# Four transformer layers on one core: the common order of 536 steps laid out anew, and buffer waits named by their own readers

## The reference

```python
x = x + tanh(gx[0]) * L0_xattn(ln(x), ctx)      # 16 heads, two softmaxes each, their difference
x = x + tanh(gf[0]) * L0_ffn(ln(x))             # three cycles of a small network that turns x
x = x + tanh(gx[1]) * L1_xattn(ctx, ln(x), mask) # 8 heads, keys from context and x
x = x + tanh(gf[1]) * L1_ffn(ln(x))             # 2 shared and 8 routed experts, best two
x = x + tanh(gx[2]) * L2_xattn(ln(x), ctx, ctx) # 16 heads
x = x + tanh(gf[2]) * L2_ffn(ln(x))             # attention, then 8 experts, best two
x = x + tanh(gx[3]) * L3_xattn(ln(x), ctx, ctx) # one head of 256
x = x + tanh(gf[3]) * L3_ffn(ln(x))             # two products with values rounded to 8 bits
```

## Time and profile before

| | |
|---|---|
| time of the runs | 5605.34, 5625.49, 5621.25 us; median 5621.25 |
| the profiled execution: its own time, its span | 5613.03 us, 5611.2 us |
| mean granted TensorE clock | 0.901 of full speed |
| busy: PE, DVE, ACT, POOL | 4673.8, 2894.8, 1919.8, 95.3 us |
| weight loads on PE | 3499.8 us, beside the matmuls |
| chain that ended last | PE 59%, DVE 27%, ACT 6%, issue 4%, DMA 3%, POOL 1% |

### The profile page before, as it was taken

How to read it: one execution, slowest core, us unless ns; L and a number is a source line. 1 busy time by engine, 2 the same in 40 slices (tenths; PEclk the granted TensorE clock), 3 DMA queues, 4 the chain that set the end, 5 groups by cost and what they waited for, 6 DMA issues and landing times.

```text
span 5611.2 us, 74711 instructions
## 1 busy us (share of the span) xinstructions
PE 4673.8 (83%) x29184; PEld 3499.8 (62%) x29184; DVE 2894.8 (52%) x7495; ACT 1919.8 (34%) x3132; POOL 95.3 (2%) x180
## 2 busy tenths in 40 slices
PE   2888878989789897898878988789887898878988
PEld 1566755667557585575855758557585575845757
DVE  4555455554555545555455454454544555455554
ACT  2433324333243333424234242342423424243242
POOL 0000000000000000000000000000000000000000
PEclk9899988989889898898978989789897998989989
DMA  6000210003000030000200002001020010200002
GB/s 254 1 15 22 105 43 1 15 22 119 29 1 23 14 121 27 1 29 23 106 27 1 29 28 101 27 1 36 23 98 27 3 34 23 98 28 12 25 23 102
DMA packets 49467, 241.04 MB, mean 43 GB/s; under 512 B 4800, under 2 KB 17088, under 8 KB 27328
## 3 DMA queue, kind: packets, MB, share of 16 engines
q1 hardware_dynamic: 49088, 235.92, 11.4%
HBM read 214.93 MB, written 20.97 MB: 42 GB/s over the span
## 4 chain that ended last, share of the span: by engine, by line
PE 59%; DVE 27%; ACT 6%; issue 4%; DMA 3%; POOL 1%; SPq 0%; DVEq 0%; ACTq 0%; another core or an unknown queue 0%
PE w L434 14%; PE w L444 9%; DVE mx L1049 7%; PE o L577 6%; PE w L693 6%; PE w L424 4%; PE w L685 4%; PE w L500 2%; PE o L570 2%; PE w L534 2%; ACT oth L805 2%; DVE stats L982 1%; PE w L549 1%; PE w L589 1%; DVE rs L995 1%
## 5 line engine op out<-in xcount | busy, mean ns | idle before, releaser
L843 ACT ACTIVATE pt<-w 128x1024 f32<-128x1024 f32 x640 | 653.3, 1023 | 560.1 <-PE w L500 316.7
L1049 DVE TENSOR_REDUCE mx<-w 128x4 f32<-128x1024 f32 x512 | 593.6, 1218 | 169.0 <-PE w L483 153.8
L577 PE MATMUL o<-pt,va 128*32 128x256 f32 x4096 | 556.0, 408 | 18.7 <-ACT pt L843 18.7
L805 ACT ACTIVATE oth<-w,res 128x256 f32<-128x256 f32 x656 | 263.5, 474 | 718.6 <-PE w L685 603.8
L434 PE MATMUL w<-xnT,stream 128*128 128x256 f32 x1792 | 426.2, 388 | 6.2 <-ACT xnT L797 6.2
L434 PEld LDWEIGHTS w<-xnT,stream 128*128 128x128 f32 x1792 | 348.0, 195 | 57.1 <-issue 7.9
L685 PE MATMUL w<-qsp,ksp 128*128 128x256 f32 x2048 | 350.9, 289 | 0.0
L577 PEld LDWEIGHTS o<-pt,va 128*32 128x32 f32 x4096 | 206.9, 113 | 191.6 <-issue 64.2
L483 PE MATMUL w<-ksp,qsp 32*128 32x256 f32 (+1 forms) x2048 | 257.9, 395 | 76.1 <-DVE mx L1049 43.8
L1019 DVE SCALAR_TENSOR_TENSOR x<-w,gate,x 128x256 f32<-128x256 f32 x512 | 224.1, 479 | 170.1 <-PE w L693 147.8
L434 PE MATMUL w<-xnT,res 128*128 128x256 f32 x896 | 280.5, 464 | 36.5 <-ACT xnT L797 27.6
(11 more groups left out here) (258 smaller groups left out, 8372.0 us busy)
## 6 DMA issues: line engine op xcount, KB each, us to landing
stream_lo<-split SPq DMA_DIRECT2D x64, 1024.0 KB, 4.8
ksp<-split SPq DMA_DIRECT2D x64, 1024.0 KB, 6.9
stream<-in_moe_dram SPq DMA_DIRECT2D x80, 384.0 KB, 3.1
stream<-in_resident_dram SPq DMA_DIRECT2D x8, 2048.0 KB, 9.0
va<-in_moe_dram SPq DMA_DIRECT2D x8, 1024.0 KB, 9.9
split<-ksp SPq DMA_DIRECT2D x8, 1024.0 KB, 5.6
split<-qsp SPq DMA_DIRECT2D x8, 1024.0 KB, 8.0
stream<-in_resident_dram SPq DMA_DIRECT2D x8, 1024.0 KB, 4.6
```

The lines of the kernel that those rows point to most:

```text
L577: mm = pe.matmul(o[g:g + 32, 0:T], by_heads(plan, s)[:, kt, plan.v_of(h), :], pt[:, n % EXPS, a * 512 + kt * T:a * 512 + (kt + 1) * T], st ...
L805: h = act.activation(dst[:, c, :], w[:, c * T:(c + 1) * T], func, bias=bias[:, c:c + 1], **more)
L843: act.activation(pt[:, n % EXPS, :], w[:, :], ACT.Exp, scale=scale).then_inc(S["s_P"], 1)
L1049: dve.tensor_reduce(mx[s][:, :, 2 * u:2 * u + 2].rearrange("p t a -> p a t"), w[:, :].rearrange("p (a t k) -> p a t k", a=2, t=TT), AX_X, ...
```

## The change

The string `ORDER` is replaced. It has the same digits, each as often as before, so every step is still done once and in the order of its own list; only the interleaving of the ten lists differs. No operation, shape or transfer is added or taken away. Three waits change: PE's wait before an `obank` is written again names the `pv` step that wrote it two items before and waits for that item's own signal; ACT's wait before a `pt` place is written again names the `exp` step that wrote it two before and waits for the `pv` that reads it; and `l3.k` waits on ACT until the last `f2.exp` of its slot is filled. `keep_item` takes the number of the buffer from the count of started items in place of that of ended ones.

```diff
 ORDER = (
-    "1016110156106000006006000005000600050550550005000500050500000550050550500500505050005000500555055055"
...
+    "6661111011605060000000000050006000050055055505000550050550000050555000000005505000005500050205550555"
+    "5055555555055055555505555550575005500050005500550702050050555505055000505050770525005050005200505005"
+    "0500050055005055050050050550555050500550050055550555555555550053505580500505080550550055005500505055"
+    "5085550530508530350000505005050050500055055000055005000500050500500505005550550555550505505050050500"
+    "0505005505005555050550500550050050000500050555055555055505505500504555555090505505509505050050550500"
+    "505050550550405550505005500550050050"
 )
...
+EXP_STEPS = steps_named(*SIGNALS["s_P"])
+ITEM_STEPS = list(ITEM)
...
                 if plan.item_starts(u) and i >= 2:
-                    pe.wait_ge(S["s_oT"], i - 1)
+                    last, ls, lu = ITEM_STEPS[i - 2]
+                    pe.wait_ge(*after("s_oT", last, ls, lu + PLANS[last[:2]].units_per_item - 1))
...
                 if n >= EXPS:
-                    act.wait_ge(S["s_pv"], n - EXPS + 1)
+                    last, ls, lu = EXP_STEPS[n - EXPS]
+                    act.wait_ge(*after("s_pv", last[:2] + ".pv", ls, lu))
...
-                bank = obank[(COUNT["s_oT"][plan.name + ".pv", s, u] - 1) % 2]
+                bank = obank[(ITEM[plan.name + ".pv", s, i * plan.units_per_item] - 1) % 2]
...
                         o = 0 if what == "q" else 2
+                        if what == "k":
+                            full(act, "f2.exp", s, F2.units - 1)
                         biased(qz[s][:, o:o + 2, :], full(act, step, s), W_["l3_b" + what], FC).then_inc(S["s_qk3"], 1)
```

More of the change, by code:

```diff
@@ L195 @@
 ORDER = (
-    "1016110156106000006006000005000600050550550005000500050500000550050550500500505050005000500555055055"
[L197 to L201, removed]
+    "6661111011605060000000000050006000050055055505000550050550000050555000000005505000005500050205550555"
+    "5055555555055055555505555550575005500050005500550702050050555505055000505050770525005050005200505005"
+    "0500050055005055050050050550555050500550550055555555555550053505580500505080550550055005500505055005"
+    "5085550530508530350000505005050050500055055000055005000500050500505005550550555550505505050505050500"
+    "0505005505005555050550500550050050000500050555055555055505550500504555555090505505509505050050550500"
+    "505050550550405550505005500550050050"
 )
```

## The result

Four runs of the changed kernel took 5525.89, 5526.36, 5531.95 and 5526.96 us, median 5526.66, beside 5616.51 for the kernel before on the same chip. The ratio is 0.9843, 95% interval 0.9822 to 0.9863: the change is faster by 1.6%, 90 us. The forecast was 5552 us; direction and range hold, the size was 61 us forecast and 90 measured.

A forecast was written before the change was run, and what follows sets the result against it. No engine is full; the order bounds the stages with waits. Terms 3.5 + 2.7 + 0 + 1.4 + 0 - 0.5 + 0.5 = 7.6 us a pass, 61 in eight, from 5613.0 to 5552 us; range 5460 to 5630.

The forecast's parts named there:

- Waits at nothing: The three changed buffer waits: same counts as the old ones or fills already done, so no time won or lost.
- Start of the pass, 3.5: Pass start to the first exp: 3.5 us a pass won, 1.9 of it from the clock; bounds 0 and 5.5.
- Signs: Profile after: `0.l0.xT` wait near 1 us, `0.l0.max:0` some 23 us after the first transpose, `shift` waits below 1 us.
- Layer 0, 2.7: Layer 0 to `f0`: a `pt` wait (1.2 us) and the `0.l0.oT` wait (1.5) go, 2.7 won.
- `f0` and the head of `l1`: 0: `0.f0.xT` to `0.l1.max:0`: two waits of 9.4 us go, new ones of 9.2 come, so 0; ends +9.4 and -14.6.
- first rival: `f0` chains overlap, no new wait shows: 9.4 us more a pass, 17.0 in all, 5477 us; chance 0.22.
- `l1`, 1.4: In `l1`, `1.l1.xT` and `1.l1.max:0` get more cover, 0.7 us each: 1.4 won a pass; bounds 0 and 1.4.
- `f1`, layer 2, `f2`: 0 in sum: `f1` begins 0, layer 2 loses 0.5 us, layer 2 to `f2` wins 0.5 a pass.
- third rival: Interleaved `f0` chains block each other: stretch of 89.0 us or more, say 96; 5669 us, slower; chance 0.14.
- second rival: Where DVE sets the pace, gains return as idle PE: start 0, layer 2 -2.5, `f2` 0; 5600 us; chance 0.18.

The follow-up runs named there:

- turn_late: Changed kernel with `1.f0.turn:0`, `1.f0.cT:1` and `1.f0.h1:1` moved behind slot 0's `f0.add` and `l1.ln`: 5630.91 us, ratio 1.0031 to the kernel before.
- old_waits: Kernel before, its three buffer waits kept, with the new `ORDER` alone: 5526.07 us, ratio 0.984 to the kernel before.
- start_only: Splice: new order for the first 89 steps (to `0.l0.exp:15`), the old order from there: 5594.82 us, ratio 0.996 to the kernel before.
- cln_moved: Changed kernel with `1.l1.cln` moved from ahead of `1.l0.norm` to behind `1.f0.ln`, and `1.l1.cT` behind `0.f0.t:1`: 5526.68 us, ratio 0.9843 to the kernel before.
- max_later: Changed kernel with the 19 steps behind `0.f2.shift:0` put back in their old sequence: 5568.2 us, ratio 0.9897 to the kernel before.
- l2_old: Changed kernel with the old order for steps 251 to 337 (`f1` and head of layer 2): 5493.17 us, ratio 0.9782 to the kernel before.
- front_only: Splice: new order for steps 0 to 250, the old order from there: 5475.18 us, ratio 0.9758 to the kernel before.

## Why the prediction was right, and where it failed

**The direction** was right, and its reason too: the order, and not an engine's work, bounds the stages with waits, and most of the waits named as dear went or shrank. `turn_late` shows that the place of the turn in the order makes its wait: 13.3 us there, 6.0 before the change, none after it.

**The total** came within the range in part by luck, since errors of opposite sign meet in it: `f0` won 8.4 us more than was said, while `f1`, layer 2 and `f2` lost 4.5 and the second context 1.3. A pass takes 679.3 us in the mean (682 was said).

**Waits at nothing:** right, as far as `old_waits` can tell.

**Start of the pass, 3.5:** 3.9 by the table, but its row ends at `1.l0.pv:0` and so holds the 1.2 us wait on `pt` that the prediction had counted under layer 0. Up to the first exponential, as the prediction had it, the start won 3.4: 1.3 idle and 2.1 busy time, near the 1.6 and 1.9 that the prediction gave without the clock and to the clock alone. With the second context's wait, which the prediction had not looked at, 2.1 to 2.2 are left: it gave the transfers no price, but the new order asks first for the context that is loaded second. Signs: `0.l0.xT` waits 1.27 (about 1 was said); the first maximum at 24.05 us in the third pass, 23.5 in the mean (23 was said). Not right: shift waits below 1 us; they are 2.30 in layers 0 and 2. And the clock did not rise through both stretches: 0.79 in the first, 0.50 in the second, where it cost little.

**Layer 0, 2.7:** the two waits went as said, on `pt` (1.2) and at `0.l0.oT` (1.5), 2.7 together. Another 2.1 us up to `1.l0.pv:12` were won in faster matmuls, which the prediction had not counted, and 0.7 were lost between the first exponential and `1.l0.exp:1`.

**"`f0` and the head of `l1`: 0"** is the step that failed. Its mechanism was right, its terms were mis-sized. The two long waits went (9.4). The new ones were given 9.2 and measure 5.9: `1.l0.oT` 3.06 in place of 4, `0.f0.cT:1` nothing in place of 1.6, `1.f0.h2:1` 0.86 in place of 2.1, `0.l1.xT` and `0.l1.vl` 0 and 1.96 in place of 1.5 together. And waits whose end I had not listed went as well: before `0.f0.h1:1` 2.41 to 0.14 us, `0.l1.xT` 1.28 to 0, `0.l1.q` 1.11 to 0, 4.7 in all. 9.4 + 4.7 - 5.9 = 8.2. The list leaves smaller waits out; all idle time together fell by 7.7 and busy time by 0.7, the 8.4 of the ledger. The stretch from `0.f0.xT` to `0.l1.max:0` alone is 75.66 us where the prediction counted 81.4, so 5.8 are won inside it and the rest beside it. The slow matmuls mostly changed places: `1.l1.vc` fell from 5.76 to 3.60 us, `1.f0.h1:1` rose from 1.89 to 3.69. So the first rival came near in this part (9.4), without being true as put: new waits do show.

**`l1`, 1.4:** 0.8. Both waits went, and 0.3 us came back at `1.l1.shift`.

**`f1`, layer 2, `f2`: 0 in sum,** forecast term by term from waits. Many waits came about as said: 4.47 at `0.f1.down:0` for 4.8, 1.21 at `1.l1.out` for 1.2, 1.12 at `1.f1.down:7` for 1.1, 2.97 at `1.f2.xT` for 2.6. Up to `0.l2.out` the loss of 1.9 us is all idle time (busy time is unchanged there). What the forecast had wrong is layer 2: `0.l2.shift:0` was to lose its wait of 2.78 us and still waits 2.30, and `1.l2.qs` waits 1.5 us in two pieces that it had not before. In the head and the scores of `f2` it is the other way round: of the 2.6 us lost there PE's busy time rose by 2.8 and its idle time fell by 0.2, for the same instructions. What was missing there is the clock behind the waits. I had used the clock as a gain at the start, where a long wait went, and not as a cost where work is spread between small waits.

The third rival (a stretch of 89 us or more) did not come; the stretch is 75.66. The second rival, that a stretch paced by DVE gives the gain back, was wrong for the start (`start_only`). It came near in layer 2 (2.5 lost were said; 1.9 with `f1`, as idle time), and not in `f2`, where the loss is busy time.

## What to carry to other kernels

When a list is laid out anew, judge it stage by stage: where two orders have done the same set of steps they can be spliced, and here the splice of the new front with the old tail beat both by 51 us and more. A wait that is moved with no queue made shorter can come up again at the next reader of the same engine (`cln_moved`). And count matmuls at the clock that they will get: less idle time made of many small waits can cost more in slow matmuls than it saves.

## What the hardware showed unasked

One kernel's runs differ with the granted clock: six runs of `max_later` took 5531.79 us at a mean clock of 0.905 and up to 5575.67 at 0.895. The Trainium skill (TensorE: Matmul & The Clock Gate, "What's actually happening") calls the point at which the clock changes run-variable; the runs agree, and they make differences below some 10 us between two of these kernels hard to read.

The lowest clock of the pass, 0.50 under the first maxima, cost little: from the first maximum to the shift the third pass of the changed kernel took 22.96 us at 0.50 and its last 22.54 at 0.56.

```profile
1477.17:1500.13 22.96, 16.15 (x85) 10.80 (x85) 19.54 (x21) 2.31 (x3) 0.00 (x0) 0.50 0.00 1
4873.31:4895.85 22.54, 15.73 (x84) 10.71 (x85) 19.53 (x21) 2.31 (x3) 0.00 (x0) 0.56 0.00 1
```

But 0.62 in place of 0.83 in `f2` cost 4.8 us of PE's busy time in the third pass (`l2_old` and `front_only`). What a low clock costs depends on who sets the pace of the stretch, and the row to read is the busy time beside the length of the stretch, not the clock alone.
